# Laying the spilled bf16 parts of q and k row-outermost in DRAM, so that a stack's partition is one run of 4096 bytes

## The reference, cut to what matters

```python
        def split(x):
            Bt, T, _ = x.shape
            return jnp.transpose(x.reshape(Bt, T, H, DH), (0, 2, 1, 3))
        Q = split(q @ Wq)
        K = split(kv @ Wk)
        V = split(kv @ Wv)
        attn = jnp.einsum('bhqd,bhkd->bhqk', Q, K) / math.sqrt(DH)
        ctx = jnp.einsum('bhqk,bhkd->bhqd', jax.nn.softmax(attn, axis=-1), V)
```

## Time and profile before

| | us |
|---|---|
| median of 3 runs | 511.99 |
| lowest and highest | 507.26, 515.48 |
| the profiled execution | 510.73 |
| its span, first to last instruction | 508.9 |
| PE busy | 393.7 (77%) |
| DVE busy | 296.2 (58%) |
| ACT busy | 216.9 (43%) |
| POOL busy | 149.4 (29%) |

### The profile page before, as it was taken

How to read it: one execution, slowest core, us unless ns; L and a number is a source line. 1 busy time by engine, 2 the same in 40 slices (tenths; PEclk the granted TensorE clock), 3 DMA queues, 4 the chain that set the end, 5 groups by cost and what they waited for, 6 DMA issues and landing times.

```text
span 508.9 us, 6721 instructions
## 1 busy us (share of the span) xinstructions
PE 393.7 (77%) x2512; PEld 266.0 (52%) x2512; DVE 296.2 (58%) x626; ACT 216.9 (43%) x473; POOL 149.4 (29%) x102
## 2 busy tenths in 40 slices
PE   2437668769887998799989888998997996684624
PEld 0402323526564677367756756675666565563613
DVE  1134144246565967497859776966776455754622
ACT  1201433553564367336735763475446546115001
POOL 4100100110444053415241722263025407235240
PEclk9999999857975899589859986987798689779556
DMA  8340240050314032303421150305030003003000
GB/s 265 144 92 1 64 81 3 20 125 1 95 52 94 6 91 73 83 12 86 117 39 52 44 135 1 95 3 135 1 95 11 2 12 82 11 1 93 10 1 11
DMA packets 35953, 29.74 MB, mean 58 GB/s; under 512 B 3536, under 2 KB 33616, under 8 KB 35792
## 3 DMA queue, kind: packets, MB, share of 16 engines
q1 hardware_dynamic: 35776, 25.86, 20.9%
q10 hardware_dynamic: 144, 3.45, 1.7%
HBM read 20.78 MB, written 8.39 MB: 57 GB/s over the span
## 4 chain that ended last, share of the span: by engine, by line
PE 39%; issue 19%; DVE 15%; POOL 10%; DMA 8%; SPq 4%; ACT 4%; POOLq 0%; ACTq 0%
DMA k_stack<-stacks 6%; POOL v_rep L764 5%; DVE top L808 4%; PE o_bank L363 4%; PE r_one L369 4%; PE h_sum L446 3%; PE r_two L501 3%; PE a_even L412 3%; PE o_bank L550 3%; PE r_one L356 2%; PE r_two L369 2%; PE a_odd L389 2%; PE h_even L434 2%; SPq L308 2%; DVE st L902 2%
## 5 line engine op out<-in xcount | busy, mean ns | idle before, releaser
L808 DVE TENSOR_REDUCE top<-a_even 128x2 f32<-128x512 f32 x64 | 44.1, 688 | 46.9 <-PE a_even L412 33.4
L626 ACT ACTIVATE probs<-h_even 128x512 f32<-128x512 f32 x64 | 38.4, 599 | 57.2 <-PE h_even L434 34.6
L412 PE MATMUL a_even<-k_stack,q_stack 48*128 48x256 bf16 x128 | 32.0, 341 | 31.5 <-DMA k_stack<-stacks 26.8
L771 POOL TENSOR_TENSOR hrs<-hvar,mhalf 128x32 f32<-128x32 f32 x8 | 44.4, 5546 | 37.0 <-DVE hvar L928 37.0
L808 DVE TENSOR_REDUCE top<-a_odd 128x2 f32<-128x512 f32 x64 | 43.6, 682 | 12.9 <-PE a_odd L412 12.9
L902 DVE TENSOR_TENSOR_SCAN st<-dec_rep,v_rep 128x1024 f32<-128x1024 f32 x16 | 40.4, 2528 | 11.6 <-ACT dec_rep L697 5.8
L626 ACT ACTIVATE probs<-h_odd 128x512 f32<-128x512 f32 x64 | 38.6, 603 | 18.5 <-PE h_odd L434 17.7
L446 PE MATMUL h_sum<-probs,v_pad 128*32 128x256 f32 x512 | 43.2, 468 | 0.0
L764 POOL TENSOR_TENSOR v_rep<-v_rep,rk 128x1016 f32<-128x1016 f32 x16 | 39.8, 2485 | 0.0
L434 PE MATMUL h_even<-q_stack,k_stack 50*128 50x256 bf16 x128 | 32.6, 346 | 5.8 <-ACT probs L626 5.3
L412 PEld LDWEIGHTS a_even<-k_stack,q_stack 48*128 48x128 bf16 x128 | 7.7, 101 | 54.1 <-DMA k_stack<-stacks 30.5
(11 more groups left out here) (159 smaller groups left out, 825.2 us busy)
## 6 DMA issues: line engine op xcount, KB each, us to landing
v_rep<-values SPq DMA_DIRECT2D x16, 511.5 KB, 5.9
W<-in_weights ACTq DMA_DIRECT2D x1, 3368.0 KB, 11.1
stacks<-parts SPq DMA_DIRECT2D x16, 192.0 KB, 2.4
q_stack<-stacks SPq DMA_DIRECT2D x16, 192.0 KB, 3.5
k_stack<-stacks SPq DMA_DIRECT2D x16, 192.0 KB, 4.5
stacks<-parts SPq DMA_DIRECT2D x16, 128.0 KB, 1.9
xin<-in_x SPq DMA_DIRECT2D x8, 128.0 KB, 2.2
xin<-in_ctx SPq DMA_DIRECT2D x8, 128.0 KB, 2.2
```

Of the source, the lines that this page charges most:

```text
L412: mm = pe.matmul(a_score[head % 2][:, j * T:(j + 1) * T], q_stack[g.p][e:e + SCORE_ROWS, head // 2, j * 128:(j + 1) * 128], k_stack[g.p][e ...
L626: act.activation(flat(probs[turn % PROBS][:, :, :]), h_score[HEAD_ORDER[turn] % 2][:, :], ACT.Exp, scale=SCORE_SCALE).then_inc(s_probs, 1)
L771: pool.tensor_tensor(hrs[:, :], hvar[:, :], mhalf[:, :], ALU.pow).then_inc(s_hrs, 1)
L808: dve.tensor_reduce(top[:, :, head], a_score[head % 2][:, :].rearrange("p (a t) -> p a t", a=2), AX.X, ALU.max).then_inc(s_top, 1)
```

## The change

The DRAM tensor `stacks` has its product row outside the channel, in place of inside it. The spill writes the same pieces of 512 bytes to other places. The columns of Wq and Wk are put in another order on the host, so that the channel index runs over (even or odd, channel in head, head pair); the eight heads of a partition are then next to each other in DRAM, and the stack's read names 4096 bytes for each partition. The read's source is now 6 product rows, a step of 32768 elements apart, by 8 channels, a step of 2048 elements apart, by 2048 elements; before it was 48 rows with one step of 256 elements (channel and product row in one), by 8, by 256. The destination is 48 partitions in both.

```diff
-        stacks = nc.dram_tensor("stacks", (2, 2, C, PRODUCTS, T), BF16, kind="Internal").ap()
+        stacks = nc.dram_tensor("stacks", (2, 2, PRODUCTS, C, T), BF16, kind="Internal").ap()
...
                         for side, which in enumerate((Q_ROWS, K_ROWS)):
                             rows = which[part]
-                            sp.dma_start(stacks[a.p, side, :, rows, :], parts[:, part, side, None, :].broadcast_to([128, len(range(PRODUCTS)[rows]), T])
+                            sp.dma_start(stacks[a.p, side, rows].rearrange("r c t -> c r t"), parts[:, part, side, None, :].broadcast_to([128, len(range(PRODUCTS)[rows]), T])
                                          ).then_inc(s_spilled[a.p], 16)
...
                     for side, dst in enumerate((q_stack, k_stack)):
                         for e in range(2):
                             sp.dma_start(dst[a.p][64 * e:64 * e + SCORE_ROWS, :, :],
-                                         stacks[a.p, side].rearrange("(i e d) r t -> e (d r) i t", e=2, d=D0)[e]).then_inc(s_stacked[a.p], 16)
+                                         stacks[a.p, side, :, 64 * e:64 * e + 64].rearrange("r (d i) t -> r d (i t)", d=D0)).then_inc(s_stacked[a.p], 16)
...
-    for n in ("Wq", "Wk", "Wv"):
-        put(n, L0[n])
+    for n in ("Wq", "Wk"):
+        put(n, L0[n].reshape(C, H0 // 2, 2, D0).transpose(0, 2, 3, 1).reshape(C, C))
+    put("Wv", L0["Wv"])
```

## The result

The changed kernel takes 533.3 us in the median (530.4 to 537.5, four runs), against 509.7 for the kernel before in the same comparison (507.3 to 515.5): a ratio of 1.049, 95% interval 1.037 to 1.060. It is slower, by 19 to 30 us. The forecast was 540 us, range 513 to 548. Medians here are of all executions; ratios and intervals leave out those that ran over 1.5% above the fastest of their kernel, so a ratio need not be the quotient of two medians.

The account below looks back on a forecast made before the run. PE's work and its wait for the last stack-read landing bound the kernel; reads growing 4.45 us in eight batches make 35.6, less a fifth 28.5, on 510.73 gives 539.2, forecast 540 us, range 513 to 548.

Parts of the forecast that it names:

- The sign and the mechanism: Stack reads: 6 outermost source rows against 48 leave six DMA engines instead of 16, so the kernel gets slower.
- The spill: Writes to the DRAM stacks: same 512-byte pieces, no time change taken, bounded at 0.1 us either side for each.
- The packet: Stack reads: 0.27 us for each 4096-byte packet, 32 an engine, so data take 8.6 us in place of 4.0.
- The nearer row: Profile row of v_rep's 4092-byte packets, 0.27 us each, preferred over the weight load's 0.164 as the price for stack reads.
- rival 1: Stack reads on six engines but with fast packets of 0.164 us: about 519 us, range 513 to 526; chance 0.28.
- The issue: SP's stack-read issues: unlike sides make each some 0.15 us longer; only the first is not hidden.
- The give-back: PE's other idle time: 0.9 us a batch, a fifth of the read's 4.45 us delay, comes back.
- my case: Stack reads on six engines at 0.25 to 0.28 us a packet: 528 to 548 us, forecast 540; chance 0.60.
- the clock: A longer wait could bring more stretches at the lower clock level: tail above 548 us, about 0.05 of the main case.
- The signs it named: Profile after: packet counts, DMA share near 6/16 over 8 us, k_stack landing 8 us or more, PE's wait up about 35.
- Rival 2: Stack reads keep 16 engines and shorten by 0.9 to 1.85 us a batch: 499 to 507 us; chance 0.11.
- The break-even of eight engines: Stack reads: at about 8 engines, 24 packets of 0.164 us take 3.9 us, against 4.0 us of data before.

## Why the prediction was right

**The sign and the mechanism.** The step on which both rested, that 6 outermost source rows against 48 leave six engines, held to the packet: six small ones a transfer. The kernel with eight engines took 1.45 of the 2.5 us out of each read again, and with sixteen engines the same long pieces are read in 5.9 us. The count was there to be read before the change, in the guard transfers.

**The spill.** Nothing, as taken; it lands in the same time.

**The packet, the term that was mis-sized.** I took 0.27 us from v_rep and left 0.164 as the low end; it is 0.19. "The nearer row" was near in size and source, and the run with 128 outermost rows bears out that the order of rows slows v_rep. But v_rep's price is one at sixteen engines, where the reads' own 4 KB packets take 0.28 us too. With six there is less traffic, which rival 1 had as its argument for itself; three quarters of the packets take 0.165 us or less, which is the low end. 32 packets of 0.19 us are 6.1 us an engine; the data run for 6.2 to 7.0 us, mean 6.6, and not 8.6, since the engines also stand idle between transfers, which the sum left out. The read grew by 2.5 us, not 4.45.

**The issue.** I took 0.15 us. The median issue grew by 0.32 (q_stack) and 0.22 us (k_stack), and the first packet starts 1.5 us after the first issue where it was 1.0, so 0.5 us later; the general form alone lengthens the read by 0.4.

**The give-back, the second miss.** I let a fifth of the delay come back. The three kernels with a longer read show the time against 8 x its growth: 3.4 us (1.0 to 5.7 by the interval) for 3.4, 11 (8 to 14) for 8.4, and 25 (19 to 30) for 20. Nothing comes back: from the profile before to the one after PE's idle time grows by 18.6 us, its wait for the stacks by 19.0, so its other waits hardly shrink. A reason could be that the engines it waits for are themselves fed by PE; no run tests that.

The misses have opposite signs, and it is luck that the time fell into the band of my case, 528 to 548. With 0.19 us a packet and all else as I had it, the read takes 1.15 + 6.1 + 0.9 = 8.15 us and the total is 524 us, which is rival 1's band. The missing give-back, the longer issue and the idle time between transfers brought it to 533. (The band's upper end was also added up short: 0.28 us and no give-back make 550.)

With 2.5 us and no give-back the sum is 510.7 + 20 = 531 us, for a profiled execution of 533.6. The two spans differ by 22.9 us: 18.6 of it is idle time of PE and 4.3 are its matmuls, longer at a granted clock of 0.812 for 0.826. The prediction had named the clock, for its tail alone. The four executions after had 0.75 to 0.81 and those of the kernel before 0.76 to 0.84, so how much of the clock's part is the change's and how much is scatter stays open.

**The signs it named.** The counts came as written, 192 packets of 4 KB and 24 small ones, the DMA share near 6/16, and the spills unchanged. PE's wait grew by 19 and not 35 us, the data ran for 6.6 us in the mean and not over 8, the last read landed 6.6 us after its issue and not 8 or more, and the issues took 0.7 us, not 0.6. A packet's mean time under 0.2 us was the sign that the size would be wrong, and it is 0.19.

**The rivals.** Rival 2's case, sixteen engines with long pieces, was built, and would not have been worth what I gave it: its read is 0.2 to 0.3 us shorter, not 0.9 to 1.85, since in both cases some 196 GB/s is all that these reads reach. The break-even of eight engines was also wrong, for the same reason that the packet was: eight are 1.05 us slower a batch, 0.4 of that by the issue.

## What to carry to other kernels

Before changing a transfer's layout, write down the outermost dimension of both sides as the instruction will carry them, and count the small packets of a transfer that has few rows there: longer pieces are no gain if they cost engines. A packet's time read from one transfer holds for its number of engines and its order of rows, not for its size alone. Where a landing is bound by rate, see whether the consumer needs all of it: two semaphores and another order of heads gave 2% where the layout cost 5%.

## What the runs showed of the hardware that I had not expected

- 786 KB into 48-partition halves take 4.1 us in pieces of 4096 bytes and 4.3 in pieces of 512 on sixteen engines; in the last batch both run at 196 GB/s.
- The same 4 KB packet takes 0.19, 0.20 or 0.28 us in the mean with six, eight or sixteen engines at work on such halves.
- Four reads in the order even, odd, even, odd half take 6.2 us, in the order even, even, odd, odd 6.8.
- 256 packets of 4092 bytes to 128 partitions take 0.27 us each when the source has 16 outermost rows and 0.20 to 0.23 when it has 128.
- An issue of the same transfer takes 0.42 to 0.47 us or 0.62 to 0.63, by the form in which it is issued; the issue of a spill of 64 partitions, cut from one of 128, takes 0.61 where the whole took 0.45.
